# A planner for an attention kernel: where score units go in short steps, when they end, and which queue moves the sums

## The reference

```
for each layer, for each of 4 batches:
    h1 = layernorm(x);  x = attention(h1, h1)  @ o1_w + o1_b + x      # 20 heads of 16, 512 keys
    h2 = layernorm(x);  x = attention(h2, ctx) @ o2_w + o2_b + x      # 20 heads of 16, 1601 keys
    h3 = layernorm(x);  a, g = split(h3 @ ff_w1 + ff_b1)              # 320 -> 2 x 1280
    x = (a * gelu(g)) @ ff_w2 + ff_b2 + x
attention: softmax(q k^T / 4) v, each head by itself
```

## Time and profile before

| | |
|---|---|
| median of 3 runs | 3419.41 us (3409.3 to 3423.13) |
| the profiled execution | 3420.76 us |
| its span, first to last instruction | 3418.9 us |
| PE, DVE, ACT, POOL busy | 90%, 60%, 56%, 21% |
| mean granted clock of PE | 0.957 of full speed |
| DMA engines, mean busy share of q1 (SP's queue) | 35.7% |

### The profile page before, as it was taken

How to read it: one execution, slowest core, us unless ns; L and a number is a source line. 1 busy time by engine, 2 the same in 40 slices (tenths; PEclk the granted TensorE clock), 3 DMA queues, 4 the chain that set the end, 5 groups by cost and what they waited for, 6 DMA issues and landing times.

```text
span 3418.9 us, 43794 instructions
## 1 busy us (share of the span) xinstructions
PE 3089.5 (90%) x16000; PEld 1395.8 (41%) x16000; DVE 2057.7 (60%) x2732; ACT 1903.0 (56%) x3646; POOL 730.7 (21%) x972
## 2 busy tenths in 40 slices
PE   4887888989999999998999999999999998998998
PEld 1332333334344433544345343453434543453445
DVE  5555556766656666655665666566765676566521
ACT  1553556656664566555664556645666466645631
POOL 3332121312302132022320333112230014002000
PEclk8997989999999999999999999999999999999999
DMA  6443334432433334334343444333244214322212
GB/s 160 136 121 102 90 84 125 136 103 56 135 97 85 108 93 133 99 106 129 95 126 85 124 118 120 105 97 113 61 130 109 69 41 134 94 51 49 69 41 77
DMA packets 208597, 342.27 MB, mean 100 GB/s; under 512 B 25464, under 2 KB 107776, under 8 KB 207104
## 3 DMA queue, kind: packets, MB, share of 16 engines
q1 hardware_dynamic: 203264, 338.09, 35.7%
q0 software_dynamic: 5120, 1.39, 0.3%
HBM read 202.29 MB, written 114.75 MB: 93 GB/s over the span
## 4 chain that ended last, share of the span: by engine, by line
PE 65%; DVE 10%; DMA 10%; ACT 6%; POOL 4%; issue 3%; SPq 2%; DVEq 0%; ACTq 0%; POOLq 0%
PE pr L1278 14%; PE po L1295 13%; DVE mx L1086 7%; PE pd L1262 7%; PE pf L1145 5%; PE pf L1198 5%; PE pf L1211 5%; PE pf L1168 4%; ACT ET L995 3%; DMA QS<-MT 3%; PE pf L1186 3%; PE pf L1177 2%; DMA raw<-ff_w_dram 2%; DMA scr_k<-HS 2%; DMA WS<-parts 2%
## 5 line engine op out<-in xcount | busy, mean ns | idle before, releaser
L995 ACT ACTIVATE ET<-pr 128x512 f32<-128x512 f32 (+1 forms) x2720 | 1478.6, 597 | 1262.2 <-PE pr L1278 1244.7
L1086 DVE TENSOR_REDUCE mx<-pd 128x2 f32<-128x800 f32 (+2 forms) x1600 | 1607.8, 1031 | 935.8 <-PE pd L1262 931.6
L1278 PE MATMUL pr<-QS,KS 64*128 64x512 f32 (+1 forms) x2720 | 862.3, 505 | 154.6 <-ACT ET L995 85.9
L1262 PE MATMUL pd<-KS,QS 64*128 64x400 f32 (+2 forms) x3200 | 684.2, 379 | 86.1 <-DVE mx L1086 67.6
L1295 PE MATMUL po<-ET,V 128*32 128x512 f32 (+2 forms) x5440 | 751.9, 626 | 0.5 <-ACT OU L1001 0.5
L1278 PEld LDWEIGHTS pr<-QS,KS 64*128 64x128 f32 (+1 forms) x2720 | 332.1, 185 | 1028.7 <-ACT ET L995 714.0
L1262 PEld LDWEIGHTS pd<-KS,QS 64*128 64x128 f32 x3200 | 375.6, 193 | 158.7 <-DVE mx L1086 117.3
L871 POOL TENSOR_TENSOR HS<-uT,HS 128x512 fp32r<-128x512 f32 (+4 forms) x168 | 190.3, 1133 | 605.0 <-ACT uT L959 604.8
L888 POOL DMA_DIRECT2D QS<-MT x160 | 94.2, 590 | 904.6 <-DVE MT L1110 902.6
L1198 PE MATMUL pf<-HS,WS 128*128 128x512 f32 x665 | 191.5, 418 | 11.3 <-issue 8.0
L1295 PEld LDWEIGHTS po<-ET,V 128*32 128x32 f32 (+2 forms) x5440 | 107.2, 108 | 215.5 <-issue 198.6
(11 more groups left out here) (81 smaller groups left out, 2054.0 us busy)
## 6 DMA issues: line engine op xcount, KB each, us to landing
WS<-parts SPq DMA_DIRECT2D x160, 320.0 KB, 3.0
QS<-scr_q SPq DMA_DIRECT2D x80, 512.0 KB, 5.6
scr_k<-HS SPq DMA_DIRECT2D x144, 200.0 KB
scr_q<-HS SPq DMA_DIRECT2D x96, 256.0 KB
KS<-scr_k SPq DMA_DIRECT2D x80, 300.8 KB, 5.2
KS<-scr_k SPq DMA_DIRECT2D x80, 300.0 KB, 6.1
KS<-scr_k SPq DMA_DIRECT2D x80, 192.0 KB, 4.7
scr_k<-HS SPq DMA_DIRECT2D x48, 256.0 KB
```

The costliest lines, as they stand in the source:

```text
L995: activation(ET[0:q.rows[k], s % 2, 2 * pair + e, :], pr[e][0:q.rows[k], :], ACT.Exp).then_inc(score_free, 1)
L1086: v.reduce_max(mx[q.kind][:, t, 2 * p:2 * p + 2, c], pd[no % 2][:, :, 0:cols], AX_X).then_inc(unit_free, 1)
L1262: ins = mm(pd[no % 2][:, e, 0:cols], queries[:, t * P:(t + 1) * P], keys, start=True, stop=True)
L1278: mm(pr[e][0:m, :], keys, queries, start=True, stop=True).then_inc(score_ready, 1)
```

## The change

Five things are changed:

1. **Short steps.** A step is called short (`all_first`) when its fill at beat 1 is under 0.9 us by the planner's table and it has none at beat 3: steps with one transpose, or with no fill. `unit_places` is 2 for beat 0 of such a step and 0 for its beat 2, so its units all stand behind the first scores. In other steps it is 1 and 1, as before.
2. **Units ended sooner.** `LAST_UNIT_AHEAD` goes from 7.0 to 9.5 us, and `_need` counts the places left only up to 6 beats ahead of the group's first step (or 8 beats behind its first unit, where that is later).
3. **Bulk loads first.** SP issues the bulk right behind the first `set_scratch`, ahead of all stores and staging.
4. **The split over 4 passes.** Layer 1's `w` jobs go beside the first 12 fills of the phases c = 1, 2, 3 and 4, five or six in each. With it, two `v2a` fills stand between the last `k2` and the first `t3`, where one stood.
5. **Moves in GpSimd's queue.** `move_rows` is POOL's, at the same beats, behind `put_maxima` and ahead of `divide`.

```diff
+W_PARTS = [(0, 6), (6, 11), (11, 16), (16, 2 * FM + 1)]
...
-        if c in (B - 1, B):
-
-            half = places("w", 1, 0, FM + 1) if c == B - 1 else places("w", 1, FM + 1)
+        if 0 < c <= len(W_PARTS):
+
             easy = 3 * TT
-            seq = mixed(seq[:easy], half) + seq[easy:]
+            seq = mixed(seq[:easy], places("w", 1, *W_PARTS[c - 1])) + seq[easy:]
         behind = places("v2a", c + 1)
         if c:
             first, rest = gate(c - 1, 4)
-            seq += behind[:1] + places("t3", c - 1) + places("g", c - 1) + [first] + rest
-            behind = behind[1:]
+            seq += behind[:2] + places("t3", c - 1) + places("g", c - 1) + [first] + rest
+            behind = behind[2:]
...
-LAST_UNIT_AHEAD, PUT_BEHIND, MOST_UNITS = 7.0, 0.5, 2
+LAST_UNIT_AHEAD, PUT_BEHIND, MOST_UNITS = 9.5, 0.5, 2
+
+BEATS_AHEAD, LEAST_BEATS = 6, 8
+SHORT_FILL = 0.9
+
+def all_first(step):
+    first, second = (sum(FILL_LENGTH.get(p[0], 0.0) for p in PLACES.get(4 * step + r, [])) for r in (1, 3))
+    return first < SHORT_FILL and not second
+
+def unit_places(beat):
+    if all_first(beat // 4):
+        return 2 if beat % 4 == 0 else 0
+    return 1 if beat % 2 == 0 else 0
...
 for _b in range(0, BEATS, 2):
+    if not unit_places(_b):
+        continue
     _now = AT[_b]
+    _next = AT[min(_b + 2 * unit_places(_b), BEATS - 1)]
     _rate, _need, _sum = 0.0, 0, 0
     for _n in sorted(n for n in _left if _left[n]):
+        if units_now(_n, _now):
+            _first_beat.setdefault(_n, _b)
+        if _n not in _first_beat:
+            continue
         _sum += units_now(_n, _now)
         _rate = max(_rate, _sum / max(UNITS_TO[_n] - _now, 0.5))
-        _need = max(_need, -(-_sum // max((4 * GROUPS[_n].step0 - 1 - _b) // 2, 1)))
-    _credit = min(max(_credit + _rate * (_now - _before), _need), max(_need, MOST_UNITS))
-    _before = _now
+        _last = max(4 * GROUPS[_n].step0 - BEATS_AHEAD, min(_first_beat[_n] + LEAST_BEATS, 4 * GROUPS[_n].step0))
+        _count = sum(unit_places(b) for b in range(_b, max(_last, _b + 2)))
+        _need = max(_need, -(-_sum * unit_places(_b) // _count))
+    _credit = min(max(_credit + _rate * (_next - _now), _need), max(_need, MOST_UNITS))
...
             sp.wait_ge(zeroed, ZEROED)
             set_scratch("q1", 0)
+            load_context(0)
+            load_x(1)
+            for which, what, l in LOAD_BEHIND[None]:
+                if which not in ("a", "b"):
+                    load_weights(which, what, l)
+            set_scratch("q1", 1)
+            for b in range(2, B):
+                load_x(b)
+            set_scratch("q2", 0)
+            set_scratch("q2", 1)
...
-                if beat == FIRST_BEAT:
-                    load_context(0)
-                    load_x(1)
...
-                if ended(beat, MOVE, MOVE_ALONE):
-                    move_rows(ended(beat, MOVE, MOVE_ALONE))
...
+            def move_rows(q):
+                pool.wait_ge(sums_out, q.n + 1)
...
+                gp.dma_start(DEN[q.kind][to, :], repeated(OU[:, :], 2 * DH, DH, DH)).then_inc(moved, 16)
...
                 for q in PUT_AT.get(beat, []):
                     put_maxima(q)
+                if ended(beat, MOVE, MOVE_ALONE):
+                    move_rows(ended(beat, MOVE, MOVE_ALONE))
```

More of the change, by code:

```diff
@@ L400 @@
 _left = {q.n: len(q.units) for q in GROUPS[1:]}
-_credit, _before = 0.0, 0.0
+_credit, _first_beat = 0.0, {}
 for _b in range(0, BEATS, 2):
+    if not unit_places(_b):
+        continue
     _now = AT[_b]
+    _next = AT[min(_b + 2 * unit_places(_b), BEATS - 1)]
     _rate, _need, _sum = 0.0, 0, 0
     for _n in sorted(n for n in _left if _left[n]):
+        if units_now(_n, _now):
+            _first_beat.setdefault(_n, _b)
+        if _n not in _first_beat:
+            continue
         _sum += units_now(_n, _now)
         _rate = max(_rate, _sum / max(UNITS_TO[_n] - _now, 0.5))
-        _need = max(_need, -(-_sum // max((4 * GROUPS[_n].step0 - 1 - _b) // 2, 1)))
-    _credit = min(max(_credit + _rate * (_now - _before), _need), max(_need, MOST_UNITS))
-    _before = _now
+        _last = max(4 * GROUPS[_n].step0 - BEATS_AHEAD, min(_first_beat[_n] + LEAST_BEATS, 4 * GROUPS[_n].step0))
+        _count = sum(unit_places(b) for b in range(_b, max(_last, _b + 2)))
+        _need = max(_need, -(-_sum * unit_places(_b) // _count))
+    _credit = min(max(_credit + _rate * (_next - _now), _need), max(_need, MOST_UNITS))
     while _credit >= 1.0:
@@ L761, in stage_group @@
                                  rows[:, e, :, first:last].rearrange("p r n -> r p n")).then_inc(keys_in[q.kind, q.at, part], 16)
[L763 to L777, removed]
             def set_scratch(k, i):
@@ L889, in put_maxima @@
                                  ).then_inc(max_in[q.n % 2], 16)
+            def move_rows(q):
+                pool.wait_ge(sums_out, q.n + 1)
+                if q.i:
+                    pool.wait_ge(fill_ready, filled("o1" if q.kind == "S" else "o2", q.i - 1))
+                if q.kind == "C" and q.i == 0 and q.g == 0:
+                    for own in scratch_set.values():
+                        pool.wait_ge(own, 16)
+                if slots_before(q):
+                    pool.wait_ge(divided[q.kind], TT * slots_before(q))
+                to = slice(64 * (q.g % 2), 64 * (q.g % 2) + 64)
+                gp.dma_start(DEN[q.kind][to, :], repeated(OU[:, :], 2 * DH, DH, DH)).then_inc(moved, 16)
+                for h in range(HG):
+                    gp.dma_start(OA[q.kind][to.start + DH * h:to.start + DH * h + DH, q.g // 2, :],
+                                 OU[32 * h:32 * h + DH, :]).then_inc(moved, 16)
             def divide(q):
```

## The result

| | before | changed |
|---|---|---|
| median | 3420.89 us (3409.3 to 3423.13, 4 runs) | 3463.39 us (3457.04 to 3472.22, 4 runs) |
| ratio, 95% interval | | 1.0124 (1.0095 to 1.0153) |
| profiled execution, span | 3420.76, 3418.9 us | 3472.22, 3470.4 us |
| mean granted clock of PE in it | 0.957 | 0.950 |

I had said 3321 us, in a range of 3284 to 3402, with 0.09 for slower. It was wrong in sign and size. The rows of after stand against those of before; the profiled execution is the slowest of the four changed ones, 9 us over their median.

The account below looks back on a forecast made before the run. PE, busy 90% of the span, was taken to set the time; short steps 22, units ended sooner 36, start 4, split 20, second `v2a` 13 and moves 4 sum to 99 us off 3420.8, giving 3321 us, range 3284 to 3402.

Parts of the forecast that it names:

- the moves: 400 DMAs of the groups' sums go from SP's queue to POOL's; nothing waits, gain 4 us, bounds +236 and -8.
- POOL's queue decides: Rival, 9%: moves hold up splits or norms in POOL's queue; share s of 236 us reaches PE, 3463 us at s = 0.6.
- my three signs: Wrong if POOL's new DMAs issue at 2 us and more, PE's `pd` wait grows over 30 us, or DVE's moves wait passes 17.6.
- The rival's second way to its end: In POOL's queue: the same slower end reached at s = 0.15 if a move costs 2 us to issue.
- Units ended sooner: Ahead of groups' scores: PE's waits for POOL's row of maxima shrink, gain 36 us, bounds 15 and 52.
- the waits only change their name: Rival, 15%: PE's waits for the maxima become waits for `pd`, and ACT gives the short steps back; 3376 us.
- Short steps: Both units ahead of the second pair fill PE's wait in about 150 steps: gain 22 us, bounds 0 and 33.
- The split: Layer 1's split jobs spread over four passes, so ACT waits less for `raw`: gain 20 us, bounds 10 and 25.
- The 56 to 59 us for the 13 steps: Sign: the 13 steps at the head of phases c = 2 and c = 3 take 56 to 59 us in both windows.
- The second `v2a`: Between last `k2` and first `t3`: the last store of keys gets another 4.4 us; gain 13 us, bounds 8 and 16.
- The start: Bulk loads first: the first wait for maxima shrinks 6.5 us, staging comes 2.5 us later; net gain 4 us.
- POOL's issues: Sign: POOL's new DMAs issue at 0.6 us each and POOL is busy near 970 us.

Follow-up runs that it names:

- moves_sp: The changed kernel with the sums' moves back in SP's queue, all else as changed: 3401.16 us, ratio 0.9943 to the kernel before.
- no_threes_end_as_before: Changed kernel with moves back at SP, short steps' need rounded down against third units, and units ending as before: 3432.6 us, 1.0045 to the kernel before.

## Why the prediction was wrong

The step that failed is **the moves**: "DVE's inversion comes 9 beats behind the moves [...], and in a full phase the margin is over 5 us, so nothing waits", a gain of 4 us. It cost 62 us (75 on the kernel before). The 9 is wrong to begin with: with the moves 8 beats behind a group's end and the inversion 14 behind, it is 6. Nine beats is its distance from the copy to `OU`, some 10.8 us at 4.8 us a step; from `OU` to the landing POOL's moves took 10.3 us in the median and 22.2 at most. I took the margin from SP's side, where a move starts 0.03 us behind `OU`, and asked only what would stand behind the moves in POOL's queue. What stands ahead of them decided: in 35 of 80 groups they start over 5 us late, and with the landing behind it the margin is gone. "I take the end near nothing because POOL sits idle two thirds of the time" was the wrong row to choose by: the idle share is an average and says nothing of one beat. In the timeline POOL works without a pause from 1302.0 until the moves are out, though it is idle for 73% of the span. The price has two parts that I had put at nothing: PE's idle time (44 of 62 us between the profiled executions) and the clock that falls with it (18 us more of busy time). In the first ten groups I had seen DVE wait for the moves and called POOL quicker there. POOL holds the moves for a shorter time (2.6 us for the five against 4.4), but comes to them up to 13 us late.

The rival "POOL's queue decides" (9%) gave 3463 us at s = 0.6, and the time was 3463. That was luck in the number: its mechanism, splits and norms held up behind the moves, isn't what most of the loss comes from. With the moves still in POOL's queue, and DVE's inversions and POOL's divisions 4 beats later, 36 of the 62 us came back. It was the last of my three signs, DVE's wait past 17.6 us, that told it. The other 26 us weren't divided further, and this rival may hold for some of them; DVE still waits 20 us more for the moves there than with SP's. The rival's second way to its end was also summed wrongly: 0.15 of 800 us on 3321 is 3441, not 3463.

**Units ended sooner** (36 us): nothing. The waits for `QS<-MT` went as I said and further, 68.0 to 21.2 us with the moves at SP. But I set the price at 0, between -10 and +12, and it was all of the gain: 24.5 us of waits for DVE and 36 for staged keys and queries against 60.3. That was the rival "the waits only change their name", with half of the new wait in a place that I had not looked at.

**Short steps** (22): 11 to 14. Empty ones and those with a `tc` were worth about what I said with two units, but 43 have three, which costs 1.1 to 1.2 us more with a transpose and 0.4 without. **The split** (20): 29 to 30 by the medians, above my bound of 25, though 25 is within the noise. The 56 to 59 us for the 13 steps missed, because these steps also wait for staged keys and queries that units ended sooner come to too early. **The second `v2a`** (13): 11 to 13, with the late `t1` as a price that I hadn't seen. **The start** (4): nothing. In the changed kernel the first scores came 5 us later.

**POOL's issues.** They took 0.5 and 0.6 us, as said, and POOL is busy for 938 us (970 said). The Trainium skill (SBUF — State Buffer, the "DVE blocks DMA" trap, and the section "A bandwidth-pool intuition that's wrong" for the figure) gives about 3.1 us, in place of 0.62, for a DMA that GpSimd issues under a DVE `tensor_copy`. The issues show nothing of it: 320 of L911 took 0.484 to 0.537 us, with DVE busy 59% of the time. Nor does that trap explain the late landings above: in the second timeline DVE stood idle from before the issues to the landing (19.03 us), in the first for the last 6.65 us. Whether any DVE operation here is of the kind that the page means, no run shows.

**What is left.** The parts don't add up. Undone one at a time from `moves_sp`, split, `v2a` and short steps are worth 54 us, but `moves_sp` is only 20 us under the kernel before. The other 34 us are in edits together, or in the rest of the planner's loop, which no run undid alone. `no_threes_end_as_before` shows that planner edits can cost 33 us jointly. I can't say more from these runs.

## What to carry to other kernels

When a DMA moves from one engine's queue to another, don't weigh it by how long it takes to issue or by how idle the engine is: list what stands ahead of it in the new queue at that beat, add the landing, and compare with the beat at which its reader comes to it; in an in-order queue such as DVE's here, a late input holds all the work behind it. A wait at a group's scores that goes because its units end sooner can come back ahead of the next units, so sum all waits of the engine that bounds, and not the one that the edit aims at. Look at the granted clock and at PE's busy time beside its waits: stalls of a few us cost more than their own length here. Try edits of a planner together as well as alone: here their gains did not add.

## What the runs showed of the hardware that I had not expected

- Five small DMAs in a row take POOL 2.6 us in the median, SP 4.4 us: as an issuer of these copies POOL is the faster one, and yet the slower choice. The rows of L911 in the changed kernel (least, median and most ns of one issue):

```profile
L911 POOL DMA_DIRECT2D OA<-OU x320: 484/487/537, 114.2 to 3362.6; - x160
```

- The same four copies of 16 rows land 3.9 us behind their last issue in the median, and 10.5 us at most; in the timeline above it was some 9 us, beside six stores from SP's queue. An issue time says little of when the data is there.
